# Routed tiles of a mixture-of-experts stage, cut into three parts of four, two and two groups instead of two parts of six and two

## The reference

```python
scores = sigmoid(xf @ gate_w.T + lb_bias)            # 8 experts
topw, topi = top_k(scores, 2)                        # 2 of them for each token
topw = topw / (topw.sum(-1) + 1e-8)
for e in range(8):
    m = topi == e
    wmean = (topw * m).sum() / max(m.sum(), 1)       # one weight per expert, over ALL tokens
    out += where(m.any(-1), mlp(xf, expert e) * wmean, 0)
out += mlp(xf, shared expert)                        # silu(x @ g.T) * (x @ u.T) @ d.T, inner size 128
```

## Time and profile before

| | us |
|---|---|
| median of 3 runs | 1465.17 (1465.15 to 1466.98) |
| the profiled execution | 1463.91 |
| its span, first to last instruction | 1462.1 |
| PE busy (matmul) | 1128.7 (77%) |
| DVE busy | 875.5 (60%) |
| POOL busy | 546.8 (37%) |
| ACT busy | 463.2 (32%) |
| mean granted clock of PE | 0.900 of full speed |

### The profile page before, as it was taken

The page is one execution under the profiler, slowest core; times in us unless marked ns, Lnnn a source line. Parts: engine busy times, 40 slices in busy tenths (PEclk is TensorE's granted clock), DMA queues, the critical chain, the costliest instruction groups (busy, mean ns, idle before and its releaser), DMA issues. The chain is left out here.

```text
span 1462.1 us, 21814 instructions
## 1 busy us (share of the span) xinstructions
PE 1128.7 (77%) x7496; PEld 851.1 (58%) x7496; DVE 875.5 (60%) x2210; ACT 463.2 (32%) x825; POOL 546.8 (37%) x982
## 2 busy tenths in 40 slices
PE   4889876492995895898599589589859979979850
PEld 2445555462863764676486477467638756757630
DVE  5788737554754763765475376376547674545563
ACT  4576543222213311412231231142223133523310
POOL 3244242046126325333632642543372212013375
PEclk9899888695998997999799799889979998999985
DMA  6544321501001301201030130121001062225574
GB/s 151 157 138 130 119 99 60 209 1 57 16 1 48 108 1 37 85 32 37 20 102 1 37 112 5 36 77 44 24 28 59 30 220 87 89 67 177 169 239 143
DMA packets 83771, 118.80 MB, mean 81 GB/s; under 512 B 28816, under 2 KB 63888, under 8 KB 81488
## 3 DMA queue, kind: packets, MB, share of 16 engines
q1 hardware_dynamic: 76752, 98.53, 20.8%
q0 software_dynamic: 6912, 18.88, 4.1%
HBM read 66.39 MB, written 51.00 MB: 80 GB/s over the span
## 5 line engine op out<-in xcount | busy, mean ns | idle before, releaser
L921 ACT ACTIVATE arena<-bank 128x512 f32<-128x512 f32 (+1 forms) x318 | 167.5, 544 | 603.2 <-PE bank L398 181.1
L398 PE MATMUL bank<-const,arena 128*128 128x128 f32 x256 | 41.4, 315 | 131.0 <-DVE arena L1402 106.0
L1428 DVE SCALAR_TENSOR_TENSOR arena<-arena,param 128x512 f32<-128x512 f32 x144 | 106.2, 749 | 38.7 <-ACT arena L944 35.0
L1307 POOL TENSOR_TENSOR arena<-arena 128x126 f32<-128x126 f32 (+22 forms) x217 | 88.0, 406 | 94.6 <-DVE arena L1519 78.7
L415 PE MATMUL bank<-hsT,wt 128*128 128x512 f32 x192 | 101.3, 686 | 26.7 <-ACT hsT L921 26.7
L398 PEld LDWEIGHTS bank<-const,arena 128*128 128x128 f32 x256 | 34.0, 162 | 135.8 <-DVE arena L1402 95.7
L649 PEld LDWEIGHTS bank<-arena 128*128 128x128 f32 x768 | 88.6, 192 | 5.8 <-issue 5.7
L1248 POOL DMA_INDIRECT slots_x<-arena x64 | 63.5, 992 | 74.3 <-DVE arena L1707 57.0
L1291 POOL COPY arena<-arena 32x128 f32<-32x128 f32 x128 | 50.4, 393 | 108.9 <-DVE arena L1509 103.0
L649 PE MATMUL bank<-arena 128*128 128x128 f32 x768 | 89.3, 275 | 0.0
L1309 POOL TENSOR_TENSOR arena<-arena 128x126 f32<-128x126 f32 (+22 forms) x217 | 81.7, 377 | 17.0
(11 more groups left out here) (263 smaller groups left out, 2715.1 us busy)
## 6 DMA issues: line engine op xcount, KB each, us to landing
arena<-slots_x SPq DMA_DIRECT2D x78, 128.0 KB, 2.1
slots_y<-arena SPq DMA_DIRECT2D x78, 128.0 KB, 1.8
xt<-x_in SPq DMA_DIRECT2D x16, 512.0 KB, 4.9
kq_T<-kq SPq DMA_DIRECT2D x8, 1024.0 KB, 3.8
kq<-kq_T SPq DMA_DIRECT2D x8, 1024.0 KB, 6.0
arena<-ffn_in SPq DMA_DIRECT2D x7, 768.0 KB, 4.2
vT<-v_T SPq DMA_DIRECT2D x8, 514.0 KB, 3.9
hs_T<-hsT SPq DMA_DIRECT2D x8, 512.0 KB, 4.3
```

What stands on the lines that cost most here:

```text
L398: last = tr(o[:, t * P:(t + 1) * P], src[:, t, c * P:(c + 1) * P], ident)
L921: free(act.activation(out_, in_, func, **kw), name)
L1307: own.link(pool.tensor_tensor(tmp, rows32[:, m0:, k].unsqueeze(2).broadcast_to([P, nm, k]), units[:, 0:k, k].unsqueeze(1).broadcast_to([P, ...
L1428: ins = V.scalar_tensor_tensor(cv[:, k % 4, :], pre[:, j, d:d + GT], param[:, at + d:at + d + 1], cv[:, k % 4, :], ALU.mult, ALU.add)
```

## The change

The groups are cut into three parts, of 4, 2 and 2 groups. That gives 39 + 23 + 23 = 85 tiles (TILE0 becomes 0, 39, 62, 85). `tiles`, `results_at` and `pads` of the first part are done in body 5 (they were in body 7, for six groups), those of the second part in body 7, those of the last part where they were. In body 5 POOL waits, ahead of its `front_solve`, until the padding rows have landed. `PIECES` now holds 24 steps, two of every three from 46 on (46, 47, 49, 50, ... 79, 80), so that 8 combines are left for after the last tile. SP's part boundary, with its words to read, comes twice: ahead of the loads of tiles 39 and 62 instead of tile 55 alone. Tables are sized by the largest part: 40 tile numbers instead of 64 (8 * NWORD8).

```diff
-PARTS = 2
-FIRST = (0, 6, NG)
+PARTS = 3
+FIRST = (0, 4, 6, NG)
...
-TILE0 = (0, NTILE[0], NTILE[0] + NTILE[1])
-
-PIECES = tuple(s for s in range(TILE0[1] + 5, TILE0[2] + 1) if s % 6)
+TILE0 = tuple(sum(NTILE[:h]) for h in range(PARTS + 1))
+PART_OF = tuple(h for h in range(PARTS) for _ in range(NTILE[h]))
+NT_ALL = TILE0[PARTS]
+
+PIECES = tuple(s for s in range(TILE0[1] + 6, TILE0[PARTS] + 1) if s % 3)[:FIRST[PARTS - 1] * T]
+assert PIECES[FIRST[1] * T] > TILE0[2]
...
             def tile_step(n):
-                if n + 1 == TILE0[1]:
-                    tile_experts(1)
+                if n + 1 in TILE0[1:PARTS]:
+                    tile_experts(PART_OF[n + 1])
...
                 if i >= 2:
                     scatter(i - 2)
-                if i == FIRST[1] + 1:
-                    pads(0)
+                if i - 1 in FIRST[1:PARTS]:
+                    pads(PART[i - 2])
                 if ahead:
                     front_rows(i + 1)
                     if i >= 2:
                         h = PART[i - 2]
                         pool.wait_ge(sem(f"scattered{h}"), 32 * T * (i - 1 - FIRST[h]))
+                    if i - 1 in FIRST[1:PARTS]:
+                        pool.wait_ge(sem(f"padded{PART[i - 2]}"), 16 * E)
                     front_solve(i + 1)
...
-                if i == FIRST[1] + 1:
-                    tiles(0)
-                    results_at(0)
+                if i - 1 in FIRST[1:PARTS]:
+                    tiles(PART[i - 2])
+                    results_at(PART[i - 2])
...
-                link(V.tensor_tensor(tot[:, 0:E], count[:, 0, :], count[:, 1, :], ALU.add))
+                link(V.tensor_reduce(tot[:, 0:E], count.rearrange("p h e -> p e h"), AX.X, ALU.add))
...
-            for n in range(TILE0[2]):
-                if n + AHEAD == TILE0[1]:
-                    part_ready(1)
-                if n + AHEAD < TILE0[2]:
+            for n in range(NT_ALL):
+                if n + AHEAD in TILE0[1:PARTS]:
+                    part_ready(PART_OF[n + AHEAD])
+                if n + AHEAD < NT_ALL:
                     load_tile(n + AHEAD)
```

More of the change, by code:

```diff
@@ L858, in tile_step @@
             def tile_step(n):
-                if n + 1 == TILE0[1]:
-                    tile_experts(1)
-                if n + 2 < TILE0[2]:
+                if n + 1 in TILE0[1:PARTS]:
+                    tile_experts(PART_OF[n + 1])
+                if n + 2 < NT_ALL:
                     rows_turned(n + 2)
-                if 0 <= n + 1 < TILE0[2]:
+                if 0 <= n + 1 < NT_ALL:
                     gate_and_up(n + 1)
-                if 0 <= n < TILE0[2]:
+                if 0 <= n < NT_ALL:
                     hidden_turned(n)
@@ L907, in _ @@
                     start=True, stop=True), n)
-            steps(TILE0[2] + 1 - at_step[0])
+            steps(NT_ALL + 1 - at_step[0])
         @block.scalar
@@ L2253, in load_tile @@
                     filled(sp, f"xT.{n - 8}")
-                sp.dma_start(xin[:, n % 8, :], slots_x[n >= TILE0[1]][bass.ds(tile_at[n] * P, P), :])\
+                sp.dma_start(xin[:, n % 8, :], slots_x[PART_OF[n]][bass.ds(tile_at[n] * P, P), :])\
                     .then_inc(sem(f"xin{n % 8}_loaded"), 16)
             def store_tile(n):
-                h = int(n >= TILE0[1])
+                h = PART_OF[n]
                 s = n - TILE0[h]
```

## The result

The changed kernel took 1474.48 us in the median of 7 runs (1471.85 to 1478.13), the kernel before beside it 1467.86 (1465.15 to 1472.24). The ratio is 1.0046, with a 95% interval of [1.0027, 1.0065]: slower by some 6.6 us (4 to 9.5 by the interval).

What follows compares the result with a forecast made beforehand. The prediction took POOL's rate of gathers to bound the tail, with the tile stage and a ring of engine waits ahead; its terms summed to +4.8 us on 1465.2, giving 1470.0 us, range 1465 to 1475 (8 in 10: 1461.5 to 1477).

Steps and rivals of the forecast that it cites:

- Tail, -17.2: After the last tile: gathers of parts 0 and 1 hide under tile steps, 15.3 us go, landing 2 us faster.
- Seven tiles, +11.4: Tile stage: seven more tiles that nothing covers, 1.63 us each, +11.4 us.
- Body 5, +3.4: Middle of body 5: DVE's table work delays PE and the engines waiting in turn by 3.4 us; padding stays hidden.
- Body 7, -1.6: Body 7: table work for two groups is shorter, so PE's wait of 1.59 us behind it goes.
- Start of the tile stage, -1.0 and -0.9: Start of tile stage: PE reads 5 words instead of 7, -1.0 us; the last `tiles` is shorter, -0.9 us.
- First boundary, +3.0: Tile 39: SP and PE read words at a second part boundary, +3.0 us, at least 1.0, at most 4.2.
- The forecast's own range: Whole kernel: 1465 to 1475 us, with bounds for stores, boundary and combines; the forecast's chance was 0.50.
- Combines, +2.7: Tile stage: nine more combines among the steps at 0.30 us each, +2.7 us.
- stores, +5.0: Tile stage: four more output stores ahead of tile loads in SP's queue, 1.25 us each, +5.0 us.
- additions for nothing: Tile stage: combines and stores fit in gaps, first boundary costs only 1.0 us; 1460.3 us, faster, chance 0.17.
- POOL as the bound in body 5: Body 5: padding DMAs start or land too late and hold up `front_solve`, some 5 us; 1475 us, chance 0.09.
- slow gathers: Tile stage: combines slow POOL's gathers, DVE and PE wait 1.6 us in 12 rounds, +19; 1489 us, chance 0.04.

Runs made afterwards that it cites:

- all three edits: Changed kernel's three parts with part 0's table work in DVE's idle slot, loads 8 tiles ahead and output stores last: 0.9891 of the kernel before, 1452.6 us.
- all four kernels traced there: Kernel before with loads 8 ahead 0.9964; parts of five and three groups, table work moved, loads 8 ahead, stores last 1.0056; changed kernel with four extra matmuls 1.0130, loads 7 ahead 1.0082.

## Why the prediction came out

The direction and, within the interval, the size were right: +4.8 predicted, +4 to +7 measured. The parts were less so, and that the sum came so near is in part luck. In the two profiled executions the difference is +10.4. Against the prediction, 0.9 of it was there before body 5, body 5 came out 2.7 too low, the start of the tile stage 2.6, the first boundary 0.9 and the tail 1.0, while the tile stage from tile 40 on was put 2.4 too high (19.1 predicted, 16.7 measured); and that last term differs by 5 us from one execution to the next.

- **Tail, -17.2:** measured -16.2. The landing took 2.5 us (2.6 predicted), the 16 gathers 18.8; 1.3 us more than before passed between the last gather and the end.
- **Seven tiles, +11.4, and no wait for gathers:** borne out. The undisturbed step stayed 1.63 us, and DVE waited for no gather between steps 46 and 80.
- **Body 5, +3.4:** measured +6.1. The mechanism was right row by row: table work of 6.9 us (7.0 predicted), PE's wait 3.51, POOL free in time, at 932.7, with 5.1 us instead of 2.2 to spare until DVE's `units` begins at 937.8. The term is mis-sized, because I let PE's delay pass on unchanged and did not ask what its clock does behind a wait of 3.5 us. Keeping PE busy left 3.45, once the time of the extra matmuls is taken off.
- **Body 7, -1.6:** PE's wait for the row behind the table work went, and the shift against before fell by 1.7.
- **Start of the tile stage, -1.0 and -0.9:** PE's words took 2.15 us instead of 3.36, and the later wait 4.42 instead of 5.34. Both came, but the first is not seen in the result of tile 0, which is 5.3 us late: a stretch of matmuls at 1198.55 took 5.33 us, where it took 3.69. Up to result 35 the shift against before is 6.0 us; with the terms as predicted behind body 7 it would be 3.4.
- **First boundary, +3.0:** measured +3.9 (result 35 to result 40), again with PE below full clock behind the wait: the matmuls that follow 1340.69 at L845 took 1.46 us, as against 1.03 undisturbed. With the loads 8 ahead 0.6 of it is left.
- **The forecast's own range:** with the bounds that I gave (0 for stores and combines, 1.0 for the boundary) the sum ends at 1460.3, and not at 1465; the 1465 had no sum behind it.
- **Combines, +2.7, and stores, +5.0:** here the reasoning failed, though 16.7 - 11.4 = 5.3 is not far from 7.7 (in the other executions it is 0 to 5.0). The 0.30 us per combine was read from five combines in six steps and taken for a price of the instruction. It was none: DVE has 1.64 us of work in a step with a combine, PE 1.63, and the kernel before with loads 8 ahead does such steps in a row in 1.64 to 1.65. In the stretch of the earlier trace rows the four longer steps (1.97 to 2.06) are those in which PE's gate and up matmuls take 1.13 us instead of 1.03. They take 1.1 us or more in 16 steps of the changed kernel from tile 40 on, and in none with all three edits, where the combines are the same and the loads 8 ahead. The waits are too short to be listed, but they go with the lead of the loads. The 1.25 us per store was a price of loads that were issued too near to their use. I named the stores as the weakest term; what I did not see is that combines, stores and boundaries draw on the same slack, the lead of 6 loads, and that this lead was the cheapest thing to change.

Of the rivals, "additions for nothing" holds for the combines and the stores with loads 8 ahead; in the kernel as changed it does not in the execution shown, since the loads are late. POOL as the bound in body 5 and slow gathers are excluded: the padding moved away changed nothing, DVE waited for no gather, and the gathers of part 1, with combines beside them, are 1.28 us apart, as against 1.25 for the last 16.

Open: which loads come late in one execution and not in another. It goes with the short lead, since the stretch takes 83.8 to 89.0 us with loads 6 ahead and 75.1 and 75.2 with 8, but what decides it for a single load was not tried. The sum of PE's waits for loads (7.2 us) is less than the 17.3 us by which the stretch exceeds 44 steps of 1.63. With loads 8 ahead 3.4 of the 17.3 are left; how the other 13.9 divide into listed waits, waits too short to be listed and the clock behind waits was not split up. Nor was it tried why the gathers slow the loads down; the medians show only that they go together.

## What to carry over

When several small additions each seem to have a price, look for the one slack that they share, here how many steps ahead a load is issued, and try that first: one number brought more than the whole change cost. Compare the lead of a load, from its issue to its first use, with the time it takes to land beside the traffic that the change puts there. When longer steps are divided by the instructions in them, the result is a price of these instructions only if the engine's own work in a step is what makes it longer. And a delay put into the middle of a ring cost its own length and the slower clock that TensorE had behind the wait, 6.6 us over the body, while the same work in a slot where the engine idles anyway cost 2.0.

## What was unexpected

In the changed kernel PE's granted clock was 1.00 up to a wait of 3.51 us and 0.50 to 0.64 for the 8 us of dense matmuls behind it; with other matmuls in the wait it stayed at 1.00. Of two executions of the same kernel, one came out of the wait at full clock for 1.13 us of matmuls and one at half at once, which made 1.3 us in body 5. And on one of the three chips the kernel before took 2% longer (1498.4 us), and all four kernels traced there show stalls of several engines at once in the tile stage that no wait in the core explains.
